# Routing twelve of sixteen batches to their own experts by an on-chip sort, in a fused two-layer attention kernel

## The reference, cut to what matters

```python
t = x * jax.lax.rsqrt(jnp.mean(x * x, axis=-1, keepdims=True) + RMS_EPS) * norm_weight
tokens = t.reshape(-1, D)
gate_logits = tokens @ gate_w.T
gate_scores, expert_idx = jax.lax.top_k(gate_logits, TOP_K)      # 2 of 8 experts
routing_weights = jax.nn.softmax(gate_scores, axis=-1)
combine = jnp.zeros((T, E), tokens.dtype).at[jnp.arange(T)[:, None], expert_idx].add(routing_weights)
def body(acc, params):
    W1, B1, W2, B2, c = params
    h = jax.nn.gelu(tokens @ W1.T + B1, approximate=False)       # 128 -> 256
    o = h @ W2.T + B2                                            # 256 -> 128
    return (acc + c[:, None] * o, None)
```

## Time and profile before

| | us |
|---|---|
| median of 3 runs (421.09 to 423.59) | 422.5 |
| span of the profiled execution | 422.1 |
| TensorE busy in it | 352.5 (84%) |
| VectorE busy | 279.8 (66%) |
| ScalarE busy | 220.8 (52%) |
| GpSimd busy | 124.8 (30%) |

### The profile page before, as it was taken

How to read it: one execution, slowest core, us unless ns; L and a number is a source line. 1 busy time by engine, 2 the same in 40 slices (tenths; PEclk the granted TensorE clock), 3 DMA queues, 4 the chain that set the end, 5 groups by cost and what they waited for, 6 DMA issues and landing times. The chain is left out here.

```text
span 422.1 us, 10432 instructions
## 1 busy us (share of the span) xinstructions
PE 352.5 (84%) x3418; PEld 255.7 (61%) x3418; DVE 279.8 (66%) x871; ACT 220.8 (52%) x426; POOL 124.8 (30%) x231
## 2 busy tenths in 40 slices
PE   1584779999978999999999999789899899746563
PEld 0353568777754777667667767557677677633342
DVE  6674768988836553662542443586778989458994
ACT  2143346776766735444344344137455575647884
POOL 6325041242532102101001001135445554521332
PEclk9977669999998999999999999859999999887999
DMA  6555964443144003620170100103444431000011
GB/s 198 141 152 111 246 163 122 143 142 121 53 143 136 2 2 62 134 54 2 37 209 17 37 0 0 37 4 117 105 117 113 116 115 59 1 2 0 26 33 44
DMA packets 54100, 34.98 MB, mean 83 GB/s; under 512 B 38744, under 2 KB 46256, under 8 KB 54064
## 3 DMA queue, kind: packets, MB, share of 16 engines
q1 hardware_dynamic: 44032, 31.43, 27.6%
q10 hardware_dynamic: 10032, 3.08, 3.0%
HBM read 24.60 MB, written 9.44 MB: 81 GB/s over the span
## 5 line engine op out<-in xcount | busy, mean ns | idle before, releaser
L1064 ACT ACTIVATE probs<-ps_e 128x512 f32<-128x512 f32 x128 | 76.1, 596 | 55.5 <-PE ps_e L899 52.1
L975 DVE TENSOR_REDUCE neg<-ps_s 128x4 f32<-128x512 f32 x128 | 86.0, 685 | 26.2 <-PE ps_s L882 24.3
L1326 DVE SCALAR_TENSOR_TENSOR x_all<-ps_ym,c_g,x_all 128x128 f32 (+1 forms) x128 | 36.0, 343 | 63.2 <-PE ps_ym L1421 63.1
L1421 PEld LDWEIGHTS ps_ym<-w,hid 128*128 128x128 f32 x512 | 60.8, 192 | 9.2 <-issue 6.7
L882 PE MATMUL ps_s<-k_rows,q_rows 96*128 96x128 bf16 x512 | 55.0, 236 | 10.8 <-DVE neg L975 4.0
L1421 PE MATMUL ps_ym<-w,hid 128*128 128x128 f32 x512 | 62.2, 276 | 0.0
L1411 PE MATMUL ps_h<-tok_t,w 128*128 (+1 forms) x128 | 61.5, 603 | 0.0
L1528 ACT ACTIVATE hid<-ps_h,b 128x512 f32<-128x512 f32 x64 | 43.2, 684 | 34.8 <-PE ps_h L1411 33.4
L882 PEld LDWEIGHTS ps_s<-k_rows,q_rows 96*128 96x128 bf16 x512 | 40.8, 106 | 25.3 <-issue 11.3
L899 PE MATMUL ps_e<-q_rows,k_rows 128*128 128x128 bf16 x512 | 52.0, 228 | 2.8 <-DMA q_rows<-neg_t 2.0
L899 PEld LDWEIGHTS ps_e<-q_rows,k_rows 128*128 128x128 bf16 x512 | 37.0, 102 | 6.5 <-DMA q_rows<-neg_t 2.7
(11 more groups left out here) (206 smaller groups left out, 548.8 us busy)
## 6 DMA issues: line engine op xcount, KB each, us to landing
k_rows<-k_dram SPq DMA_DIRECT2D x32, 144.0 KB
q_rows<-q_dram SPq DMA_DIRECT2D x32, 144.0 KB
k_rows<-k_dram SPq DMA_DIRECT2D x16, 288.0 KB
q_rows<-q_dram SPq DMA_DIRECT2D x16, 288.0 KB
k_dram<-parts SPq DMA_DIRECT2D x35, 128.0 KB, 2.4
w<-in_w SPq DMA_DIRECT2D x16, 128.0 KB, 2.7
q_dram<-parts SPq DMA_DIRECT2D x15, 128.0 KB, 2.2
q_dram<-parts ACTq DMA_DIRECT2D x9, 128.0 KB, 3.0
```

The source lines that it names most:

```text
L975: dve.tensor_reduce(neg[:, s, q * HQ:(q + 1) * HQ], ps_s[:, q % 2, :].rearrange("p (h k) -> p h k", h=HQ), AX_X, ALU.max, negate=True).the ...
L1064: act.activation(probs[:, s, q, :], ps_e[:, q % 2, :], ACT.Exp, scale=SCALE).then_inc(exp_done, 1)
L1326: dve.scalar_tensor_tensor(out=batch_of(x_all, g * G + j), in0=ps_y[:, e % 2, j * D:(j + 1) * D], scalar=c_g[:, j, e:e + 1], in1=batch_of( ...
L1421: last = pe.matmul(ps_y[:, e % 2, j * D:(j + 1) * D], hid[:, (e % 2) * M + m, j * P:(j + 1) * P], w2[:, e, m, :], start=(m == 0), stop=(m ...
```

## The change

Group 0 (four batches) still passes all eight experts. The other twelve batches (`SORTED = 12`) are sorted by expert. Each token has two copies, one for each of its experts. For each expert the number of its copies is rounded up to whole tiles of 128 rows, so at most `TILES = 31` tiles are needed, and always 31 are worked on.

The rank of each copy within its expert comes from 13 bf16 multiplications with a triangle and with ones (`count_ranks`); VectorE works out each copy's row (`place`) and the expert that owns each tile (`owner_i`). GpSimd writes the normalised tokens to their rows of `xs_dram` with 24 indirect DMAs, 128 rows of 512 bytes each. SP loads the sorted rows in fours of tiles (`load_sorted`). For each tile GpSimd loads the owner's offset into a register and copies that expert's weights, 514 values a partition, into one of four slots (`w_tile`); TensorE turns the tokens, multiplies with the slot's weights, ScalarE applies Gelu, TensorE multiplies again, VectorE copies the result out, and SP stores it to `ys_dram` (`store_sorted`). 

In the second attention GpSimd gathers each token's two results with 24 indirect DMAs in all (`gather`), VectorE adds them to `x_all` with their weights (`add_experts`), and the queries of groups 1, 2 and 3 are made there, in steps 0 to 5, where before it was group 3 alone. Group 0's queries are made beside the tiles. `w1`, `w2` and `b1` are one array, `w12`, loaded by eight DMAs in place of sixteen; `xs_dram` is cleared with one DMA of zeros. The gate logits are computed with tokens on the partitions, so that no copy and no turn follows them. Semaphores of the first stage are cleared and used again.

```diff
+SORTED = B - G
+TILES = (2 * SORTED * P + E * (P - 1)) // P
+QUAD = 4
+QUADS = -(-TILES // QUAD)
+EXPERT = HID + M * D + M
+W_SLOTS = 4
+PROJECTED = {1: 1, 3: 2, 5: 3}
...
 # experts, gpsimd
+            leave_keys(0)
+            pool.wait_ge(c["zeroed"], 16)
+            pool.wait_ge(placed, 1)
+            for b in range(SORTED):
+                for n in range(2):
+                    pool.indirect_dma_start(out=c["xs_dram"], in_=tk[:, G + b, :], in_offset=None,
+                                            out_offset=bass.IndirectOffsetOnAxis(ap=place[:, n, b:b + 1], axis=0))\
+                        .then_inc(scattered, 16)
+            for g in range(1, NG):
+                leave_keys(g)
+            flat = w12[:].rearrange("p e n -> p (e n)")
+            pool.wait_ge(owned, 1)
+            for u in range(TILES):
+                first = pool.value_load(owner_i[0:1, u:u + 1], min_val=0, max_val=(E - 1) * EXPERT)
+                wait(pool, yt_done, u - W_SLOTS + 1)
+                pool.tensor_copy(w_tile[:, u % W_SLOTS, :], flat[:, bass.ds(first, EXPERT)]).then_inc(w_ready, 1)
+                if u == 7:
+                    queries.root(pool, 0)
+                if u == 15:
+                    queries.leave(pool, 0)
...
 # experts, tensor: the dense part
             def gate(g):
                 pe.wait_ge(tok_ready, g + 1)
-                wait(pe, lg_ready, g - 1)
-                pe.matmul(ps_y[0:E, g % 2, :], gate_w[:], tok_t[:, g * GT:(g + 1) * GT], start=True, stop=True)\
-                  .then_inc(lg_done, 1)
+                for j in range(G):
+                    b = g * G + j
+                    last = pe.matmul(ps_g[:, b * E:(b + 1) * E], tok_t[:, b * P:(b + 1) * P], gate_w[:], start=True, stop=True)
+                return last
...
+            for e in range(E):
+                if e + 1 == 2:
+                    pe.wait_ge(c["expert_in"][1], 16 * (E - 2))
+                if e + 1 < E:
+                    hidden(e + 1)
+                if e < NG:
+                    context_group(e)
+                else:
+                    turn_weights(e - NG)
+                out(e)
+                if e == 0:
+                    count_ranks()
+                if e >= NG:
+                    bias(e - NG)
...
 # experts, tensor: the tiles
+            def hidden_tile(u):
+                k, r = u // QUAD, u % W_SLOTS
+                pe.wait_ge(xs_copied, k + 1)
+                pe.wait_ge(w_ready, u + 1)
+                wait(pe, hs_ready, (u - 1) * M)
+                tok = (1 + k % (NG - 1)) * GT + u % QUAD * P
+                for m in range(M):
+                    last = pe.matmul(ps_h[:, u % 2, m * P:(m + 1) * P],
+                                     w_tile[:, r, m * P:(m + 1) * P], tok_t[:, tok:tok + P], start=True, stop=True)
+                last.then_inc(hs_done, 1)
...
+            for u in range(TILES):
+                if u + 2 < TILES:
+                    hidden_tile(u + 2)
+                out_tile(u)
+                if u % QUAD == 2 and u // QUAD + 2 < QUADS:
+                    turn_sorted(u // QUAD + 2)
...
 # attention(layer=1), gpsimd
+            def gather(g, batches):
+                if g == 1 and batches[0] == 0:
+                    for r in range(QUAD):
+                        pool.wait_ge(c["ys_stored"][r], 16 * QUADS // QUAD)
+                for j in batches:
+                    for n in range(2):
+                        b = g * G + j
+                        pool.indirect_dma_start(out=yg[:, n, b - G, :], out_offset=None, in_=c["ys_dram"],
+                                                in_offset=bass.IndirectOffsetOnAxis(ap=c["place"][:, n, b - G:b - G + 1], axis=0))\
+                            .then_inc(gathered[g - 1], 16)
...
-            run(pool, step, {-1: lambda: queries.root(pool, last), 1: leave_queries} if also else {1: add_bias}, beside)
+            run(pool, step, {-3: lambda: gather(1, range(G)),
+                             -1: lambda: gather(2, (0, 1)),
+                             0: lambda: (queries.root(pool, 1), gather(2, (2, 3))),
+                             1: lambda: (queries.leave(pool, 1), gather(3, (0, 1))),
+                             2: lambda: (queries.root(pool, 2), gather(3, (2, 3))),
+                             3: lambda: queries.leave(pool, 2),
+                             4: lambda: queries.root(pool, 3),
+                             5: lambda: queries.leave(pool, 3)} if also else {1: add_bias}, beside)
...
 # attention(layer=1), vector
+            def query_piece(g, n):
+                def do(q):
+                    if n == 0 and q < 2:
+                        add_experts(g, q)
+                    if n == 0 and q == 2:
+                        dve.wait_ge(added, g * 2 * G)
+                        queries.stats(dve, g)
+                        queries.variance(dve, g)
+                    if n == 1 and q == 0:
+                        queries.normalise(dve, g)
+                    if n == 1 and q == NQ - 1:
+                        queries.split(dve, g)
+                piece[:] = [do]
...
 # attention(layer=1), sync
+                queries.store(sp, 1)
+                for b in range(G, B):
+                    if b % G == 0:
+                        sp.wait_ge(queries.stored[b // G], 16 * PARTS)
                     load(b, b % SLOTS)
+                    if b in (6, 8):
+                        queries.store(sp, {6: 2, 8: 3}[b])
```

More of the change, by code:

```diff
@@ L774, in attention @@
         block = ph.enter_context(nc.Block())
[L776 removed]
+        queries = c["q1"]
         also = layer == 1
@@ L820, in load @@
                 lay_maxima(b - 2, (r - 2) % SLOTS)
-            if layer == 1:
-                queries.store(sp, last - 1, queries.stored[0])
             for b in range(2):
@@ L1051, in beside @@
                 piece[:] = [do]
-            run(dve, step, {-2: measure_queries, -1: normalise_queries, 2: lambda: queries.split(dve, last)} if also
+            run(dve, step, {2 * g + n - 3: (lambda g=g, n=n: query_piece(g, n)) for g in range(1, NG) for n in range(2)} if also
                 else {}, beside)
@@ L1104, in step @@
                         copy_projected(b - 2, s)
-            run(act, step, {0: lambda: queries.copy_turned(act, last, ps_y[:]),
-                            1: lambda: queries.copy(act, last, ps_y[:]),
-                            **{2 + n: lambda n=n: queries.store_part(act, last, n, queries.stored[2]) for n in range(PARTS)}}
+                    if also and isinstance(b, int) and b in PROJECTED:
+                        if q == 1:
+                            queries.copy_turned(act, PROJECTED[b], ps_q[:])
+                        if q == 2:
+                            queries.copy(act, PROJECTED[b], ps_q[:])
+            run(act, step, {}
                 if also else {-3: lambda: (store_unit(act, c, LATE[0], c["parts_stored"]),
@@ L1237, in _ @@
                 load_rows(sp, c, 1, b, b)
-            queries.store(sp, 1, queries.stored[1])
+                store_sorted(QUAD + b)
         @block.gpsimd
@@ new lines, in _, with copy_out @@
+            dve.wait_ge(y_read, E * G)
+            dve.wait_ge(b_read, NG)
+            queries.stats(dve, 0)
+            queries.variance(dve, 0)
+            for g in range(1, NG):
+                split_keys(g)
+            def copy_out(k):
+                last = k * QUAD + tiles_of(k)
+                dve.wait_ge(yt_done, last)
+                wait(dve, c["ys_stored"][k % QUAD], 16 * (k // QUAD))
+                dve.tensor_copy(ys[:, k % QUAD, 0:tiles_of(k) * D], ps_y[:, k % 2, 0:tiles_of(k) * D]).then_inc(ys_copied, 1)
@@ L1359, in _ @@
+            copy_out(0)
+            queries.normalise(dve, 0)
+            copy_out(1)
             qs.settle()
@@ new lines, in out_tile @@
+            def out_tile(u):
+                k, r = u // QUAD, u % W_SLOTS
+                pe.wait_ge(hs_ready, (u + 1) * M)
+                if u % QUAD == 0:
+                    if k < 2:
+                        pe.wait_ge(y_read, E * G)
+                    wait(pe, ys_copied, k - 1)
+                for m in range(M):
+                    last = pe.matmul(ps_y[:, k % 2, u % QUAD * D:(u % QUAD + 1) * D], hid[:, u % 4, m * P:(m + 1) * P],
+                                     w_tile[:, r, HID + m * D:HID + (m + 1) * D], start=(m == 0), stop=(m == M - 1))
+                last.then_inc(yt_done, 1)
@@ L1561, in _, with copy_weights @@
-            group(0, first=True)
-            with act.Fori(1, NG) as g:
-                group(g)
+                                   bias=w12[:, e, HID + M * D + m:HID + M * D + m + 1]).then_inc(h_ready, 1)
+            def copy_weights(g):
+                act.wait_ge(ct_done, g + 1)
+                wait(act, b_done, g)
+                act.activation(c_t[:], ps_c[0:E, :], ACT.Copy).then_inc(ct_ready, 1)
+            for g in range(NG - 1):
+                copy_tokens(g)
+            activate(0)
@@ L1566, in ternary_ffn @@
```

(8 more changed lines are left out.)

472 lines of the change are left out of this document (268 added, 204 removed).

## The result

The changed kernel takes 454.73 us (median of 4 runs, 454.01 to 455.98) where the kernel before takes 422.16 beside it. The ratio is 1.077, with a 95% interval of 1.074 to 1.080: slower by 7.7%. I had forecast 413.5, with a range to 434. Its profiled execution has a span of 454.2 us.

The account below looks back on a forecast made before the run. The expert stage was taken as bound by TensorE, busy throughout. From a 422.1 us span, 37.9 us gained there and 29.2 us lost in the second attention gave 413.4, forecast 413.5 us, range 398 to 434.

Parts of the forecast that it names:

- Gating and places: Expert stage start: logits ready at about 137.1 us instead of 139.10, choosing done at 141.0, places known at 146.9.
- The price of an indirect DMA: Scatter in the expert stage: 1.2 us for each of 24 GpSimd DMAs, 28.8 us in all, ending at 175.7.
- Rival A: Scatter and gathers: an indirect DMA holds GpSimd for 2.0 us, total 440.6 us; chance 0.17.
- So the sort is hidden behind the dense batches at 1.2 us a DMA.: Expert stage: GpSimd's scatter and k remainders end at 179.3 us, before TensorE's dense part at 183.9.
- the 24 scatters end before TensorE's dense part does: Expert stage: a sign that the forecast is right, with the scatters ending before the dense part, near 184 us.
- Tiles: Expert stage: 1.22 us a tile on TensorE, 1.4 on GpSimd, running nearly level from 188 us; stage ends at 232.5.
- rival B: Tiles: the register load is a round trip, 2.0 us or more a tile, total 427.8 us; chance 0.13.
- rival D: Tiles: TensorE idles so much that its clock falls, plus 15 us or more, total 430; chance 0.03.
- The chain to batch 4: Second attention: GpSimd's queue, split, stores and load put batch 4's scores 41.3 us in, before 20.6; 20.7 us lost.
- VectorE 7, clock 1.5: Second attention: 7 us lost to VectorE's added work in steps 2 to 5, 1.5 us to TensorE restarting at low clock.
- my own case: Whole kernel: the forecast of 413.5 us, with its own range of 405 to 424; chance 0.45.
- Rival C: Gathers: cheap indirect DMAs at 0.6 us give back 9.6 us, expert stage unchanged, total 404; chance 0.22.

Follow-up runs that it names:

- e2: Changed kernel with its 24 scatters as plain DMAs from GpSimd, rows in order instead of by place: 430.36 us, 1.017 of the kernel before.
- e3: Changed kernel with the 24 scatters as plain DMAs issued by SP's queue instead of GpSimd's: 430.29 us, 1.016 of the kernel before.
- e4: Changed kernel with all 24 scatters held until VectorE has added the last dense expert: 466.9 us, 1.104 of the kernel before.
- e13: Changed kernel with one 128x512 GpSimd fill behind each scatter, one scatter per 1.68 us: 443.9 us, 1.048 of the kernel before.
- e14: Changed kernel with two 128x512 GpSimd fills behind each scatter, one scatter per 2.25 us: 457.6 us, 1.078 of the kernel before.
- e5: Changed kernel with the second attention's 24 gathers replaced by six plain loads on SP's queue: 445.98 us, 1.053 of the kernel before.
- e6: Changed kernel with the query stores of groups 2 and 3 placed later in SP's list: 450.33 us, 1.066 of the kernel before.
- e7: Changed kernel without indirect DMAs (plain GpSimd scatters, six plain SP loads for gathers) and with two query stores later: 418.56 us, 0.990 of the kernel before.
- e16: Changed kernel with a 128x512 fill behind each scatter, later query stores, earlier tile turns and a split zero fill: 436.58 us, 1.033 of the kernel before.
- e9: Changed kernel with four tiny GpSimd fills (128x1) behind each scatter: 453.1 us, 1.070 of the kernel before.

## Why the prediction was wrong

In its own order, against the profiled span of 454.2 us:

- **Gating and places.** Forecast: logits at 137.1, places at 146.9. Measured 142.24, and the first scatter at 151.09. I had taken 2 us off for the copies and turns and had worked out nothing else. The stage begins 1.7 us later, the clock is lower (0.61 granted up to the logits, 0.84 before), and `hidden(0)`, 3.57 us there, stands ahead of the last logits. By itself this cost nothing, since TensorE had dense work to do.
- **The price of an indirect DMA.** Forecast 1.2 us, measured 1.27, so 30.3 us for 24 and not 28.8. Right. Rival A (2.0 us) did not happen: 0.96 us are on GpSimd and 0.30 behind it. By the Trainium skill, page "DMA: Bandwidth & Descriptors", section "Anatomy of one DMA — SWDGE (gpsimd) path", a GpSimd DMA has some 2.0 us of fixed cost; the trace shows that they don't hold the queue.
- **The step that failed: "So the sort is hidden behind the dense batches at 1.2 us a DMA."** I asked only whether the dense work is as long as the scatter. It is: forecast to end at 183.9 us, it ends at 179.6 to 182.4 wherever it isn't held up (e2, e3, e4, e13, e14). That this is so near is in part luck. Work started later than I said, and experts 4 to 7 take 19.2 us (162.07 to 181.26 in e2) where I put 23.6; the rows that I named for them add up to 22.3. But 24 indirect DMAs at 1.27 us slow down the work that was to hide them, by 22.5 us, of which TensorE stands 16.1 and works at a lower clock for the rest. It was done at 205.6. This is 21.7 of the 41 us between forecast and time. That I said the trace of before has no such row should have made me ask for a rival in which the cover itself suffers; I had none. My signs could not have shown it either: "the 24 scatters end before TensorE's dense part does" came true (181.43 and 205.63), and says nothing about when the dense part ends.
- **Tiles.** Forecast from the dense part's end 48.6 us, measured 50.0. The register load was priced too high (0.90 us a tile with the copy, and 0.57 where no tile is waited for, instead of 1.4), and rival B is refuted. GpSimd is busy for 20.33 of 50.00 us and so is not level with TensorE (37.34), as I had thought. What that gave was taken back on TensorE, which waits up to 1.39 us for ScalarE at every fourth tile. The clock stayed full (rival D refuted).
- **The chain to batch 4.** Forecast +41.3 us, measured +44.0, 2.7 off, with the links in the order that I gave. But I took GpSimd's queue, with 19 us of gathers in it, for all that sets it. Without them (e5) it is 34.5, so behind the queue stands a second chain only 9.5 us shorter, which I hadn't priced.
- **"VectorE 7, clock 1.5."** Mis-sized. From the scores of batch 4 to the stage's end it is 99.3 us instead of 76.0: 23.3 lost, where I gave 8.5. e6 and e7 split it: 4.4 us are SP's list, in which it stands at a query store ahead of loads that are due; 18.0 are the five steps that carry queries, 2.3 to 4.6 us longer each than the 6.01 of the earlier trace rows. I had set VectorE's spare time in a step (6.01 less 3.91) against the new work. In a step with additions VectorE needs 9.84 us, not 3.91 and 4.0; in one with a projection, charged 0.5 us, no engine is full, and the work comes as a chain through four engines which process their lists in order. For the clock I gave 1.5 us, once; it stays lower throughout (0.90 granted over the 99.3 us, 0.98 before), and its share is not measured.

The sum: 21.7 in the dense part, 1.4 in the tiles, 17.7 in the second attention (2.7 and 14.8, less rounding) over 413.4 make 454.2. Either of the two large terms alone would have put the time at 431 or more, above my own case, which ended at 424, and made the kernel slower. The runs show it for the second attention: with the dense part on time the sort still loses, by 1.7% in e2, which gives up the row order, and by 3.3% in e16, which has all of the work.

Rival C (cheap indirect DMAs, 404) did not happen either, and would not have given 404: with plain scatters at 0.54 us each and no gathers on GpSimd the time is 418.6, with the row order given up.

What stays open is what exactly the engines lack while indirect DMAs follow each other closely. The rows say "issue" and "remote", on three engines at once, with the DMA engines 0.15 busy; they begin some microseconds after the first scatter and not with it; and in e9 GpSimd joins them for 4 us in the middle of a row of fills. That fits a late supply of instructions, which is an argument and not a measurement. The Trainium skill, page "Runtime: NRT & Kernel Launch", section "Instruction fetch mechanics", says that each sequencer fetches its instructions by a DMA queue of its own, in blocks of 16 KiB, "mostly hidden"; the page of the profile counts 21 and 18 packets of such queues, but no view gives their times, so no run here shows that they were late. The run with a loop, meant to settle it, was confounded by its pauses.

## What to carry to other kernels

A cover has two sides: ask whether the work that hides a new operation is long enough, and also whether it keeps its own speed beside it. If an operation has no row in the trace, the second question is open, and deserves its own rival.

If engines that have nothing in common stand still together, at instructions without a wait, and go on together, look for what the idle-looking engine does at that time, and test it by spacing it out: 0.5 us of filler behind each scatter made this kernel 11 us faster.

Work that is handed through four engines inside a sequence of steps can cost its chain, and not the busy time of its busiest engine: here 2.3 to 4.6 us a step instead of the 0.5 to 3 that the spare time suggested.

## What the runs showed of the hardware

- Beside 24 indirect DMAs (128 rows of 512 bytes), one per 1.27 us for 30.3 us, TensorE's work of 32.05 us took 22.5 us longer: it stood 16.1 us, and the rest is lower clock (0.78 granted on average). At one per 1.38 us it took 17.7 longer, at one per 1.68 or 2.25 us nothing. TensorE kept its pace for the first 14.7 us of them. The same number of plain DMAs of the same size at 0.54 us from GpSimd did no harm, nor did they from SP at 0.50.
- An indirect DMA holds GpSimd for 0.96 us, a plain one of the same rows for 0.54.
- Up to four tiny fills (0.20 us in all) between two indirect DMAs are nearly free: they stand in the 0.30 us that separates them anyway, and the spacing goes from 1.27 to 1.32 us.
